# A graph attention layer on one core: three pairs of h0 transposed by DMA, row scores in three parts

## The reference, cut to what matters

```python
h0  = maximum(layernorm(x), 0)                       # called h in the reference
type_sum = adj @ h0
attn_a = sigmoid(concat([type_sum, h0]) @ Wa.T + ba)  # attn_b likewise with Wb, bb
h = h0 @ W_sa
s_left, s_right = h @ a_sa[0, :256], h @ a_sa[0, 256:]
e = where(adj != 0, exp(-leaky_relu(s_left[:, None] + s_right[None, :], 0.01)), 0)
x_a = (e / (sum(e, axis=1) + 1e-5)) @ h
x_b = adj @ (h0 @ W_gcnb) + b_gcnb
out = x + sigmoid(attn_a * x_a + attn_b * x_b)
```

## Time and profile before

| | us |
|---|---|
| runs: median (lowest to highest) | 178.64 (178.15 to 179.17) |
| the profiled execution | 178.25 |
| its span, first to last instruction | 176.4 |

### The profile page before, as it was taken

The page is one execution under the profiler, slowest core; times in us unless marked ns, Lnnn a source line. Parts: engine busy times, 40 slices in busy tenths (PEclk is TensorE's granted clock), DMA queues, the critical chain, the costliest instruction groups (busy, mean ns, idle before and its releaser), DMA issues.

```text
span 176.4 us, 3397 instructions
## 1 busy us (share of the span) xinstructions
PE 171.6 (97%) x1324; PEld 125.8 (71%) x1324; DVE 147.0 (83%) x309; ACT 115.4 (65%) x169; POOL 18.6 (11%) x42
## 2 busy tenths in 40 slices
PE   7999999999999999999999999999999999999992
PEld 2556776654444468888844488888888888888892
DVE  3799997648999999799999922999999999976551
ACT  3679899642899988748494640675875884863310
POOL 4745436030000200000000000000000000000000
PEclk9999999999999999999999999999999999999999
DMA  5999996999991598000001100000010010011101
GB/s 129 288 260 260 224 181 116 202 206 211 298 423 43 82 214 180 0 4 2 0 4 59 59 0 4 0 0 0 4 59 0 6 59 0 4 61 59 60 33 30
DMA packets 5520, 16.87 MB, mean 96 GB/s; under 512 B 625, under 2 KB 1409, under 8 KB 4737
## 3 DMA queue, kind: packets, MB, share of 16 engines
q0 software_dynamic: 1584, 8.39, 24.6%
q1 hardware_dynamic: 3920, 8.27, 13.2%
HBM read 22.94 MB, written 2.11 MB: 142 GB/s over the span
## 4 chain that ended last, share of the span: by engine, by line
PE 94%; DMA 3%; DVE 1%; SPq 1%; issue 0%; ACT 0%; DVEq 0%
PE ps L773 31%; PE ps L815 16%; PE ps L816 16%; PE ps L814 16%; PE ps L751 6%; PE ps L807 6%; DMA wa_sb<-in_w_wide 3%; PE ps L745 2%; SPq L234 1%; PE ps L877 0%; DVE wa_hi L507 0%; DVE logit L724 0%; DVE e_lo L526 0%; ACT logit L411 0%; DVE res L631 0%
## 5 line engine op out<-in xcount | busy, mean ns | idle before, releaser
L814 PE MATMUL ps<-mv_lo,e_hi 128*128 128x257 f16 (+2 forms) x272 | 71.0, 267 | 0.0
L816 PE MATMUL ps<-mv_hi,e_lo 128*128 128x257 f16 (+2 forms) x272 | 70.8, 266 | 0.0
L815 PE MATMUL ps<-mv_hi,e_hi 128*128 128x257 f16 (+2 forms) x272 | 70.8, 266 | 0.0
L377 ACT ACTIVATE z<-z,log_e 128x1024 f32<-128x1024 f32 x32 | 36.7, 1146 | 29.1 <-DVE z L568 29.1
L568 DVE SCALAR_TENSOR_TENSOR z<-sl_row,exs,far 128x512 f32<-128x512 f32 x64 | 45.0, 743 | 0.0
L576 DVE TENSOR_TENSOR e_lo<-z,e_hi 128x1024 f16<-128x1024 f32 x32 | 38.9, 1216 | 1.2 <-ACT e_hi L387 1.2
L773 PE MATMUL ps<-adj,nat_lo 128*128 128x512 f16 x128 | 36.8, 379 | 0.0
L773 PE MATMUL ps<-adj,nat_hi 128*128 128x512 f16 x128 | 36.7, 379 | 0.0
L387 ACT ACTIVATE e_hi<-z 128x1024 f16<-128x1024 f32 x32 | 33.3, 1041 | 0.0
L815 PEld LDWEIGHTS ps<-mv_hi,e_hi 128*128 128x128 f16 x272 | 26.5, 98 | 3.2
L814 PEld LDWEIGHTS ps<-mv_lo,e_hi 128*128 128x128 f16 x272 | 26.4, 97 | 3.3
(11 more groups left out here) (69 smaller groups left out, 164.8 us busy)
## 6 DMA issues: line engine op xcount, KB each, us to landing
adj<-in_adj_t POOLq DMA_DIRECT2D x6, 1024.0 KB, 10.4
x_sb<-in_x SPq DMA_DIRECT2D x6, 512.0 KB, 8.9
out<-res SPq DMA_DIRECT2D x7, 256.0 KB, 2.0
adj<-in_adj_t POOLq DMA_DIRECT2D x3, 512.0 KB, 7.5
x_sb<-in_x SPq DMA_DIRECT2D x3, 256.0 KB, 4.8
sl_row<-sl_line SPq DMA_DIRECT2D x1, 768.0 KB, 9.7
adj<-in_adj_t POOLq DMA_DIRECT2D x2, 256.0 KB, 5.9
wa_sb<-in_w_wide SPq DMA_DIRECT2D x1, 258.0 KB, 4.5
```

What stands on the lines that cost most here:

```text
L377: act.activation(z[:, n % ZRING, :, :], z[:, n % ZRING, :, :], ACT.Exp, bias=log_e[:, 0:1], scale=SLOPE - 1.0).then_inc(exp_done, 1)
L814: pe.matmul(ps[:, bank, cols], e_hi[:, s, i1], mv_lo[:, j, cols], start=(j == 0), stop=False)
L815: pe.matmul(ps[:, bank, cols], e_hi[:, s, i1], mv_hi[:, j, cols], start=False, stop=False)
L816: return pe.matmul(ps[:, bank, cols], e_lo[:, s, i1], mv_hi[:, j, cols], start=False, stop=(j == NT - 1))
```

## The change

The transposes of units 6, 7 and 8 (pairs 5, 6, 7) leave TensorE. SP issues for each pair two DMA transposes of 128 x 512 fp16, from the halves nat_hi and nat_lo in SBUF to h0t_hi and h0t_lo, once these halves are ready and the last adjacency piece of chunk 0 has landed; the layout of h0t becomes tile, k, column for that. The wide products of the three pairs go into the second aggregate, behind its tiles 7, 11 and 15, and wait for the DMA transposes. Their mv_highs, mv_lows and narrow_results move into the n loops. The row scores go in three parts (tiles 0 to 3, 4 to 7, 8 to 15), the first two transposed ahead of wide(3) and wide(5), the third in the third aggregate; the copies of them lie in c_sb. GpSimd issues some adjacency pieces earlier and waits for all six DMA transposes ahead of those of chunk 2. SP waits for an adjacency piece of chunk 2 before it loads x again, and half_added moves to n = 8, 9, 11 and 12.

```diff
...
 NU = len(UNITS)
-SL_PARTS = ((0, 4), (4, 16))
-SL_UNIT = 4
-SL_BANKS = (2, 0)
+SL_PARTS = ((0, 4), (4, 8), (8, 16))
+SL_UNITS = (3, 5)
+SL_BANKS = (6, 6, 0)
...
 X_PARTS = ((0, 1), (1, 2), (2, 4), (4, 6), (6, 8), (8, 12), (12, 16))
-WIDE_BANKS = (6, 2)
...
+LATE = 3
+ONTIME = NPAIR - LATE
+NTURN = NU - LATE
+WIDE_BANKS = (6, 2, 6, 2, 6, 2, 0, 2)
 B_BANKS = (4, 6, 4, 4)
-ADJ_PIECES = ((0, 0, 2), (0, 2, 4), (0, 4, 8), (0, 8, 12), (0, 12, 16), (1, 0, 8), (1, 8, 16), (2, 0, 8), (2, 8, 16), (3, 0, 8), (3, 8, 16))
+ADJ_PIECES = ((0, 0, 2), (0, 2, 4), (0, 4, 6), (0, 6, 8), (0, 8, 12), (0, 12, 16), (1, 0, 8), (1, 8, 16), (2, 0, 8), (2, 8, 16), (3, 0, 8), (3, 8, 16))
...
-        h0t_hi = e_hi[:, 16:24, :].rearrange("p (k s) n -> p k (s n)", k=KT)
-        h0t_lo = e_lo[:, 16:24, :].rearrange("p (k s) n -> p k (s n)", k=KT)
+        h0t_hi = e_hi[:, 16:24, :].rearrange("p s (a k n) -> p (s a) k n", k=KT, n=P)
+        h0t_lo = e_lo[:, 16:24, :].rearrange("p s (a k n) -> p (s a) k n", k=KT, n=P)
...
-        sl_turn = [part_b[0:hi - lo, h, 0:P] for h, (lo, hi) in enumerate(SL_PARTS)]
+        sl_turn = [c_sb[0:hi - lo, C_WT + h * P:C_WT + (h + 1) * P] for h, (lo, hi) in enumerate(SL_PARTS)]
...
         h0t_ready = sem("h0t_ready")
+        h0t_landed = [sem(f"h0t_landed{p}") for p in range(ONTIME, NPAIR)]
...
         sl_moved = sem("sl_moved")
-        sl_stored = [sem(f"sl_stored{h}") for h in range(2)]
-        sl_ready = [sem(f"sl_ready{h}") for h in range(2)]
+        sl_stored = [sem(f"sl_stored{h}") for h in range(3)]
+        sl_ready = [sem(f"sl_ready{h}") for h in range(3)]
...
             n = (UNITS[u][1] - UNITS[u][0]) * P
-            return ps[:, u % 2, 0:KT * n].rearrange("p (k n) -> p k n", k=KT)
...
-        def h0t_cols(tile, u):
-            return tile[:, :, UNITS[u][0] * P:UNITS[u][1] * P]
+            return ps[:, u % 2, 0:KT * n].rearrange("p (t k n) -> p t k n", k=KT, n=P)
...
+        def h0t_tiles(tile, u):
+            return tile[:, UNITS[u][0]:UNITS[u][1], :, :]
...
         def wide_bank(t):
-            return WIDE_BANKS[t // 2 % 2] + t % 2
+            return WIDE_BANKS[t // 2] + t % 2
...
             load_x(5)
-            sp.wait_ge(x_landed[4], 16)
+            sp.wait_ge(adj_landed[1], 16)
...
+            def turn_by_dma(p):
+                ts = slice(2 * p, 2 * p + 2)
+                for have, nat, h0t in ((nat_high, nat_hi, h0t_hi), (nat_ready, nat_lo, h0t_lo)):
+                    sp.wait_ge(have, p + 1)
+                    sp.dma_start(h0t[:, ts, :, :].rearrange("p t k n -> p (t k) n"),
+                                 nat[:, ts, :].rearrange("p t d -> p (t d)"),
+                                 transpose=True).then_inc(h0t_landed[p - ONTIME], 16)
...
             sl_spread(0)
+            sp.wait_ge(adj_landed[piece_of(0, NT - 1)], 16)
+            turn_by_dma(ONTIME)
+            turn_by_dma(ONTIME + 1)
             sl_store(1)
-            sp.wait_ge(turned, NU)
+            turn_by_dma(ONTIME + 2)
+            sl_spread(1)
+            sp.wait_ge(adj_landed[piece_of(2, 0)], 16)
+            sp.wait_ge(turned, NTURN)
...
                 sp.dma_start(x_sb[:, ts, :], x[:, ts, :]).then_inc(x_back[g], 16)
-            sl_spread(1)
+            sl_store(2)
+            sl_spread(2)
...
             load_adj(2)
+            load_adj(3)
             norms(3)
-            load_adj(3)
+            load_adj(4)
             norms(4)
-            load_adj(4)
+            load_adj(5)
             norms(5)
+            load_adj(6)
             norms(6)
-            load_adj(5)
...
             norms(8)
-            load_adj(6)
             load_adj(7)
+            for p in range(ONTIME, NPAIR):
+                pool.wait_ge(h0t_landed[p - ONTIME], 32)
             load_adj(8)
+            load_adj(9)
...
             pool.wait_ge(far_ready, JP)
-            load_adj(9)
             load_adj(10)
+            load_adj(11)
...
                 act.wait_ge(turned, u + 1)
-                act.activation(h0t_cols(h0t_hi, u), turn_bank(u), ACT.Copy).then_inc(h0t_high, 1)
+                act.activation(h0t_tiles(h0t_hi, u), turn_bank(u), ACT.Copy).then_inc(h0t_high, 1)
...
                 act.wait_ge(exs_ready, p + 1)
-                if p == SL_UNIT - 1:
-                    sl_lines(0)
+                if p + 1 in SL_UNITS:
+                    sl_lines(SL_UNITS.index(p + 1))
...
             for p in range(1, NPAIR):
-                if p + 1 < NPAIR:
+                if p + 2 < NTURN:
...
                     nat_highs(p + 2)
-                mv_highs(p)
-            act.activation(factor_l[:, :], exs[:, :, SL], ACT.Exp, scale=SLOPE).then_inc(factors_done, 1)
+                if p < ONTIME - 1:
+                    mv_highs(p)
+            mv_highs(ONTIME - 1)
             agg_highs(0)
-            sl_lines(1)
...
                     act_high(n - 1)
-                if n in (2, 3, 4):
-                    half_added(n - 2)
-                if n == 6:
+                if n == 2:
+                    mv_highs(5)
+                if n == 3:
+                    mv_highs(6)
+                if n == 5:
+                    mv_highs(7)
+                    act.activation(factor_l[:, :], exs[:, :, SL], ACT.Exp, scale=SLOPE).then_inc(factors_done, 1)
+                if n == 7:
                     agg_highs(1)
-                    half_added(3)
+                if n == 8:
+                    sl_lines(2)
+                if n in (8, 9, 11, 12):
+                    half_added((8, 9, 11, 12).index(n))
...
                 dve.wait_ge(h0t_high, u + 1)
-                dve.tensor_tensor(h0t_cols(h0t_lo, u), turn_bank(u), h0t_cols(h0t_hi, u), ALU.subtract).then_inc(h0t_ready, 1)
+                dve.tensor_tensor(h0t_tiles(h0t_lo, u), turn_bank(u), h0t_tiles(h0t_hi, u), ALU.subtract).then_inc(h0t_ready, 1)
...
                 if j == 0:
-                    dve.wait_ge(sl_ready[min(c, 1)], 16)
+                    dve.wait_ge(sl_ready[min(c, 2)], 16)
...
                 dve.wait_ge(far_ready, n + 1)
+                if ONTIME <= n < NPAIR:
+                    dve.wait_ge(exs_ready, n + 1)
...
             mv_lows(0)
-            for p in range(1, NPAIR):
-                if p + 1 < NPAIR:
-                    nat_lows(p + 1)
+            for p in range(1, ONTIME - 1):
+                nat_lows(p + 1)
...
                     mv_lows(p - 1)
-                if p + 4 < NU:
-                    moments(p + 4)
+                moments(p + 4)
                 narrow_results(p)
-                if p + 1 < NPAIR:
-                    h0t_lows(p + 2)
-            mv_lows(NPAIR - 1)
+                h0t_lows(p + 2)
+            moments(NU - 1)
+            nat_lows(ONTIME)
+            mv_lows(ONTIME - 2)
+            narrow_results(ONTIME - 1)
+            for p in range(ONTIME + 1, NPAIR):
+                nat_lows(p)
+            mv_lows(ONTIME - 1)
...
                     dve_low(n - LAG)
-                if n == 7:
+                if n == 2:
+                    narrow_results(5)
+                if n == 3:
+                    mv_lows(5)
+                    narrow_results(6)
+                if n == 4:
+                    mv_lows(6)
+                if n == 5:
+                    narrow_results(7)
+                if n == 6:
+                    mv_lows(7)
+                if n == 8:
...
                     for k in range(KT):
-                        cols = slice((t - UNITS[u][0]) * P, (t - UNITS[u][0] + 1) * P)
-                        ins = pe.transpose(turn_bank(u)[:, k, cols], x_sb[:, t, k * P:(k + 1) * P], ident[:, :])
+                        ins = pe.transpose(turn_bank(u)[:, t - UNITS[u][0], k, :], x_sb[:, t, k * P:(k + 1) * P], ident[:, :])
...
                     for k in range(KT):
-                        ins = pe.matmul(ps[:, wide_bank(t), cols], h0t[a][:, k, t * P:(t + 1) * P], wa2[b][:, k, cols],
+                        ins = pe.matmul(ps[:, wide_bank(t), cols], h0t[a][:, t, k, :], wa2[b][:, k, cols],
...
             def wide(u):
-                pe.wait_ge(h0t_ready, u + 1)
+                if u < NTURN:
+                    pe.wait_ge(h0t_ready, u + 1)
+                else:
+                    pe.wait_ge(h0t_landed[u - NTURN], 32)
...
                         pe.wait_ge(mv_ready, t - 3)
-                    if t == UNITS[SL_UNIT][0]:
-                        sl_lines(0)
+                    if u in SL_UNITS and t == UNITS[u][0]:
+                        sl_lines(SL_UNITS.index(u))
...
                 if j0 == 0 and c == 1:
-                    pe.wait_ge(mv_ready, NT - 2)
+                    pe.wait_ge(mv_ready, 2 * ONTIME)
...
                 if p == 0:
-                    pe.wait_ge(sl_moved, 2)
+                    pe.wait_ge(sl_moved, 3)
...
                 b_pair(p)
-                if p + 1 < NPAIR:
+                if p + 2 < NTURN:
                     turn(p + 2)
-                wide(p + 1)
-            b_products(1, 0, 4)
-            pe.wait_ge(h0t_ready, NU)
```

(15 more changed lines are left out.)

## The result

The changed kernel takes 177.56 us (median of 22 executions, 176.57 to 179.31) against 178.75 us of the kernel before, measured beside it (22 executions, 177.73 to 179.55). The ratio is 0.9926, with a 95% interval of 0.9909 to 0.9943: 1.3 us faster. The forecast was 177.4 us, with faster as the likeliest case.

What follows compares the result with a forecast made beforehand. TensorE's own instructions were taken to bound the kernel from about 10 us on. Removing 1.32 us and adding 0.11 takes the span from 176.4 to 175.2 us, profiled 177.0, median 177.4; range 176.8 to 180.2.

Steps and rivals of the forecast that it cites:

- The sum of 1.21 us on TensorE: Three turns of 0.44 us leave TensorE (1.32 us), one score transpose of 0.11 us is added: 1.21 us less.
- calendar: TensorE's predicted start times after the change, used as other engines' due times; first attention products at 63.05 us, not 64.26.
- Up to the product of pair 3 nothing moves: TensorE's early part keeps its times, except that the first score transpose comes 3.5 us earlier.
- thin covers: Small spare times before TensorE's due times: 0.8 us at the third score copy, 0.6 us at the last transpose's upper end.
- Store to spread: On SP's queue, the first score row's store was taken to need 4.67 us before its spread could go.
- Last landing: Pair 7's DMA transposes were to land at 34.6 us, or 40.8 us by the upper end of landing times.
- the limit: Latest landing of the last transpose that costs nothing: 49.17 - 7.8 = 41.4 us.
- The hold: GpSimd waits for the last transpose before the third aggregate's pieces: free until 41.4 us, one for one after.
- Third copy: ScalarE's copy of the third score part, done at 62.1 to 62.3 us, due 63.05 at the first attention product.
- (b): Rival: a thin cover gives (third score copy, halves or a transpose), TensorE waits 0.3 to 1.5 us; 177.8 to 179.0; chance 0.26.
- (d): Rival: last transpose lands between 42.6 and 45 us, TensorE waits 1.2 to 3.6 us; 178.7 to 181.1; chance 0.10.
- (c): Rival: the DMA transposes don't overlap, the last lands at 52.9 us, 11.5 us of TensorE wait; about 189 us; chance 0.12.

Runs made afterwards that it cites:

- e9: The kernel before with only the change's new order of the front's DMAs; 178.27 us, ratio 0.9955 to the kernel before.
- e10: The changed kernel with the front's DMA order of the kernel before; 177.68 us, ratio 0.9945 to the kernel before.
- e4: The changed kernel plus six more unread DMA transposes of the same size, late, at about 87 us; 178.06 us in one execution.
- e2: The changed kernel with two more DMA transposes that GpSimd also waits for before chunk 2's pieces; 181.29 us over all ten executions.
- e5: The changed kernel with the first row-score part transposed ahead of wide(4), as in the kernel before, not wide(3); 177.85 us, ratio 0.9935.
- e8: The kernel of e7 with pair 4 also transposed by DMA, turn(5) leaving TensorE; 177.74 us, ratio 0.9911 to the kernel before.
- e3: The changed kernel without GpSimd's wait for the DMA transposes ahead of chunk 2's pieces; 187.75 us, ratio 1.0474 to the kernel before.
- e6: The changed kernel with ScalarE's third score copy one step later, n = 9 instead of 8; 184.06 us, ratio 1.0244 to the kernel before.
- e7: The changed kernel with the first DMA transpose pair ahead of the first score row's spread and the third score part earlier; 177.4 us, ratio 0.9882.

## Why the prediction was right

**The time and the sum.** Forecast 177.4 us, measured 177.56. The sum of 1.21 us on TensorE is confirmed: by its calendar (1.19 us from the first aggregate to the first attention product), and by the turns put back (1.0 to 1.3 us). That the median came out within 0.2 us is in part luck, by the next two points.

**A step that was missing.** "Up to the product of pair 3 nothing moves" took the front's DMA order as worth nothing. In the profiled execution that is true; over many executions it is worth 0.8 us in the median by e9, where most long executions are gone, though e10 doesn't confirm it and what made them long is open. The prediction rested on one execution, 0.39 us below the median, in which no piece was late, and carried its distance to the median over unchanged; the changed kernel's profiled execution (176.94 us) is 0.6 us below its median. The two parts add up to 0.97 + 0.84 = 1.8 us; the two comparisons of the changed kernel gave 1.3 and 1.9. Whether the parts add or some of the first is given back through thin covers can't be told within these intervals.

**The transposes.** The steps were right in kind and sizes were off. Issue: 0.4 us taken, 1.2 to 2.2 measured. Store to spread: 4.67 us taken, 6.7 measured. Last landing: 34.6 us taken, 40.8 the upper end, 40.5 measured. The forecast survived only because of its upper end: the limit, taken as 41.4, is 49.01 - 7.5 - 0.54 = 41.0 us, with the 0.54 us that GpSimd needs from the landing to its first issue. 0.5 us were left of 6.8 that the taken values gave. And that was one execution: in e4's the same kernel was 0.6 us behind the limit. That the cover held often enough for the gain to show was luck in its size.

**The hold.** "So the hold is free until ... and costs one for one after that": the wait is shown by e2, and in part by e4, e5 and e8. What the prediction didn't ask is what the hold buys. Without it the kernel is 10 us slower (e3). It costed the wait and overlooked its use.

**The later chain.** Third copy at 62.1 to 62.3 taken, 62.66 measured, due 62.93. The row landed at 35.4, taken as "by 34". That the place is on the path from there on is shown by e6.

**The rivals.** (b) and (d) name the right places: TensorE waited there 0.6 us in e4, which is the same kernel so far, and 3.3 us in e2, 0.8 us in e5 and in e8, 4.3 us in e6. Their price was put at one for one. That fits the short waits (e4, e5, e8), behind which the products kept full speed; behind the long ones the granted clock makes it more (e2, e3, e6). (c), with serial transposes, is excluded by e4. Its other reason, DMAs beside adjacency pieces, is what the hold keeps away.

## What to carry to other kernels

Where one engine carries the chain, give each instruction moved off it a due time and each helper's queue a calendar; here that gave the time to 0.2 us, and the places that most of the later experiments broke. Cost a DMA by its issuing engine too: a transpose of 128 x 512 fp16 held the issuing queue 1.2 to 2.7 us here, and one that was issued beside megabytes of other loads held it for 11, so keep those loads back until it has landed. And look at the spread of executions as well as at one profile: a gain can lie in the executions that were not profiled. Where a wait is named as the cause, look up when it was: a wait for "the adjacency" at 16 us and one at 50 us have different causes.

## What the runs showed of the hardware

- SP stood 11.34 us in the issue of one DMA transpose while three 1 MB pieces of the adjacency were queued (e3), of which the changed kernel has one there; without queued work it takes 1.27 us (e4).
- TensorE waits of 3.3 us (e2), 4.3 us (e6) and 8.3 us (e3) were followed by half clock (1.2 GHz) for some 3.3, 5 and 5 us after the return, which cost 1.6, 2.6 and 2.6 us on top of the wait. Behind waits of 0.6 and 0.8 us at about 50 us (e4, e5, e8) the clock stayed full. In the first 16 us it fell in some executions and not in others with the same waits (0.75 over 12 to 16 us in e9; 1.00 over 8 to 14 us in e10).
- 128 KB transposed from SBUF to SBUF lands in 2.4 to 2.5 us with little beside it, in 3.3 to 7.5 us in the changed kernel, and in 17.2 us in e3.
- The store of the first score row (2 KB, to DRAM) let its spread go 4.7 us after its issue in the kernel before, 6.7 us in the changed one, and 10 us with two DMA transposes issued behind it (e7).
